# A four-layer model on one core: first weights loaded a stage ahead, a scatter moved over a stage boundary, B and C rows read from four copies

## Chip, cores, metric

The kernel runs on one core of one Trainium2 chip. The metric is the device time of one launch in microseconds (us), median of the runs.

## The reference

Four layers of an attention-like part and a feed-forward part, each followed by a residual sum and a layer norm, on a state of 2048 tokens by 1024 channels, in float32. Cut to the parts that the change touches:

```python
# layer 0, feed-forward: channels permuted, 16 small MLPs, permuted back
t = x.reshape(b*l, Dm)[:, perm].reshape(b*l, h, d)
t = gelu(einsum('bhd,hdm->bhm', t, up)); t = einsum('bhm,hmd->bhd', t, down)
x = layernorm(x + t.reshape(b*l, h*d)[:, unperm])
# layer 1, attention: a convolution of 3 taps gives q, k, v; attention in blocks of 128
c = conv(x, conv_w) + conv_b; q, k, v = split(c, 3)
qh, kh, vh = q@wq + bq, k@wk + bk, v@wv + bv            # 16 heads of 64
... softmax in each block ...; y = (o@wo + bo)@proj_w + proj_b
x = layernorm(x + y)
# layer 2, "attention": a selective scan, 2048 channels, 16 states
ssm_p = einsum('bdl,ed->ble', xc, x_proj_w)             # dt (64), B (16), C (16), each rms-normed
h = exp(dt*A)*h + dt*B_t*x_t                            # for each t, channel, state
y_t = sum over states of h*C_t
# layer 3, attention
qkv = x@Wqkv + bqkv                                     # 1024 -> 3*256
```

## The kernel before, in words

The state (`state`, `K.X`) stays in SBUF, channels on the partitions: 8 tiles (`KT`) of 128 channels by 2 x 1024 tokens. Work goes in chunks of 512 tokens (`NT`), of which there are 4 (`CHUNKS`). The program is a row of stages; each is a block in which the five instruction queues (SP for DMAs, POOL, TensorE, VectorE, ScalarE) run their own written-out order and meet by semaphores. Between blocks all engines meet. After a layer's part `recycle` (L68) clears the semaphores and all engines meet again. A stage's tiles and weights live in that stage alone, so each stage's SP queue starts with the loads of its own weights.

**Layer 0.** `l0_attn` (L1029) runs the attention, then one block for the output projection `L0Out` and the feed-forward `L0Ffn`. SP there loads `up`, `down` and then, as soon as a chunk has been scattered, that chunk back from DRAM (`Unpermute.load`, L1183). POOL first gathers the rows of the output weights (`l0out_rows`, L982), which TensorE turns (L996) before it can project. The permutation back is done by scatter: for each chunk eight indirect DMAs from POOL (`Unpermute.scatter`, L1176, issued at L1180) write the chunk's rows to DRAM in their final order. The scatter of chunk i waits for that chunk's last scaling (`ln.done`, VectorE L138). The last chunk's load stands in the convolution's SP queue.

**Convolution** (`conv`, L1203). 6 output tiles (m) times 2 batches give 12 units of 28 us. For each m SP loads the outer taps into `G` (L1235, L1236) and the middle tap into `mid` (L1239); ScalarE halves `mid` (L1270), VectorE adds the outer taps (L1288) and makes two more weight tiles (L1291, L1292). VectorE makes the input pieces `V` (L1302 to L1304), with a ring of 4, eight for a unit. TensorE multiplies at L1255, L1256 (outer taps) and L1260, L1261 (made tiles). Unit 1 needs chunks 2 and 3 of the state.

**Block attention** (`block_attention`, L1333). SP loads four biases (L1375) and `wq`, `wk`, `wv`, `wo` (L1376 to L1379), 1 MB each. TensorE waits for the biases, then for `wq`.

**Layer 2.** `l2_inproj` (L2251) projects and convolves; at its end the 128 rows of normed dt, B, C of each chunk (in `sq`) are stored to `l_ssm` in DRAM (L2295), and SP waits for these stores. `l2_scan` (L2477) goes through 4 chunks x 16 channel tiles (`ct`) = 64 items (q), each of 8 steps of two states. POOL makes `dtx*B` of a step (L2772, three steps ahead), VectorE scans (L2842), then the product with C is done by VectorE in five of eight steps (L2853) and by POOL in three (L2797). TensorE sums the states (L2676), and in between computes the gate (L2666) and the output projection of earlier chunks (L2463). B and C must lie on all 128 partitions: `rows` (L2582) loads two rows of one chunk from DRAM into `Bb` or `Cb` with a source that repeats for every partition, 512 KB a load, 16 loads a chunk. There is one buffer for a chunk's rows, so group g of chunk c+1 is loaded once the last item of chunk c has used group g.

**Layer 3.** `l3_project` (L3003): SP loads `W` in eight row blocks (L3019), the first tile waits for each of them (L3032).

Of the kernel before, what the change touches and what calls it, by code (L numbers as in the profile page):

```python
# [23 lines left out]
P = 128  # L24
# [1004 lines left out]
def l0_attn(nc, K, w, w_ffn, back):  # L1029
    with Stage(nc, "l0") as s:  # L1030
        o = Holder()
        o.oT = s.sb("oT", [P, GROUPS, T])
        with Stage(nc, "l0qkv") as s1:
            o.hi = s1.sb("hi", [P, 2, T], F32R)
            o.lo = s1.sb("lo", [P, 2, T], F32R)
            o.v = s1.sb("v", [P, T // P, HEADS, HP])
            a = L0Attn(nc, K, w)
            with Stage(nc, "l0proj") as s2:
                a.project(s2, o)
            with Stage(nc, "l0att") as s2:  # L1040
                a.attend(s2, o)
        with Stage(nc, "l0pair") as s1:
            pair = Pair(s1, K, 2, ())
            with Stage(nc, "l0out") as s2, Stage(nc, "l0ffn") as s3:
                pair.run(nc, L0Out(s2, K, w, o.oT, pair), L0Ffn(s3, K, w_ffn, back, pair))
# [17 lines left out]
class L0Ffn(DenseLN):  # L1063
# [6 lines left out]
    def __init__(self, s, K, w, back, pair):  # L1070
        super().__init__(s, K, pair=pair, first=CHUNKS, banks=slice(4, 6))
        self.w, self.back = w, back
# [9 lines left out]
    def sync(self, e):  # L1082
# [72 lines left out]

class Unpermute:
# [19 lines left out]
    def scatter(self, g, i, done, n):  # L1176
        g.wait_ge(self.rows_ok, CHUNKS)
        g.wait_ge(done, n)
        for k in range(KT):
# [23 lines left out]
def conv(nc, K, w, qkv, back):  # L1203
# [5 lines left out]
    with Stage(nc, "l1conv") as s:  # L1209
        G = s.sb("G", [P, 2, 4, KT, P])  # L1210
        mid = s.sb("mid", [P, KT, P])
# [6 lines left out]
        w_in = [s.sem(f"w_in{j}") for j in range(2)]  # L1218
        mid_in = s.sem("mid_in")
# [2059 lines left out]
```

## Time and profile before

| | |
|---|---|
| median of 3 runs | 5426.35 us (5425.6 to 5430.8) |
| the profiled execution | 5436.66 us |
| its span, first to last instruction | 5434.9 us |
| TensorE busy | 4925.0 us (91%) |
| VectorE busy | 3253.0 us (60%) |
| ScalarE busy | 2120.0 us (39%) |
| POOL busy | 2304.8 us (42%), nearly all of it in the scan, 2400 to 4330 us |
| mean granted TensorE clock | 0.953 |
| DMA | 358 MB, mean 66 GB/s |

A share over the whole span says little here, since the stages have different limits: each place that the change touches has to be read from its own stretch. Times in the rows are microseconds from the start of the span. PE is TensorE, DVE VectorE, ACT ScalarE, POOL GpSimd, SPq the queue of SyncE with the DMAs that it issues.

### The profile page before, as it was taken

The page shows a single profiled execution, that of the slowest core. Times are in us where ns is not written, and L with a number is a line of the kernel's source. Part 1 is how long each engine was busy: PE and PEld are TensorE (multiplying, and loading weights), DVE is VectorE, ACT ScalarE, POOL GpSimd, SP SyncE. Part 2 cuts the span into 40 slices and gives each one's busy share as a digit, 9 for nine tenths or more (in the row PEclk, how much of TensorE's full clock was granted, in tenths as well). Part 3 has the DMA queues.
Part 4 walks back from the last instruction along what each step waited for, and adds up shares of the span by engine and source line. Part 5 has one row for each costly group of instructions (what it writes and reads, how often), then busy time and mean ns, then how long its engine had stood idle before and what let it go on. Part 6 is the DMA issues. An engine that isn't in the chain of part 4 may idle for free. (4 is left out here: it accounts for less than half of the span.)

```text
span 5434.9 us, 40419 instructions
## 1 busy us (share of the span) xinstructions
PE 4925.0 (91%) x14496; PEld 2357.8 (43%) x14496; DVE 3253.0 (60%) x3534; ACT 2120.0 (39%) x2856; POOL 2304.8 (42%) x1219
## 2 busy tenths in 40 slices
PE   8998879989868899967888999999999999899998
PEld 4443224467626444423333444444344344456443
DVE  1663458845457323238998999899899822103522
ACT  1454620045333211135665666666566521102211
POOL 1003420000032100019998999999899842100421
PEclk9898989999979999988999999999999999999999
DMA  2001030000010022132116445544744320000001
GB/s 74 1 1 55 31 116 35 12 32 1 8 33 1 28 70 70 54 96 62 41 36 154 134 135 143 169 128 125 175 135 135 120 93 0 23 0 13 35 16 47
DMA packets 174758, 358.21 MB, mean 66 GB/s; under 512 B 18590, under 2 KB 52510, under 8 KB 170462
## 3 DMA queue, kind: packets, MB, share of 16 engines
q1 hardware_dynamic: 166494, 327.82, 20.2%
q0 software_dynamic: 8064, 27.80, 1.4%
q8 instruction: 116, 1.90, 0.1%
q14 instruction: 84, 0.69, 0.0%
HBM read 299.98 MB, written 55.57 MB: 65 GB/s over the span
## 5 line engine op out<-in xcount | busy, mean ns | idle before, releaser
L2772 POOL TENSOR_TENSOR l2scan_h<-l2scan_dtx,l2scan_Bb 128x1024 f32<-128x1024 f32 x512 | 1199.7, 2362 | 73.2 <-DMA l2scan_Bb<-l_ssm 56.7
L2676 PE MATMUL l2scan_yp<-l2scan_h,ident 128*128 128x512 f32 x2048 | 984.9, 615 | 134.6 <-POOL l2scan_h L2797 122.6
L2741 ACT ACTIVATE l2scan_ring<-l2scan_dt,l2scan_A 128x512 f32<-128x512 f32 x1024 | 661.3, 681 | 506.1 <-DVE l2scan_h L2853 399.6
L2676 PEld LDWEIGHTS l2scan_yp<-l2scan_h,ident 128*128 128x128 f32 x2048 | 393.1, 195 | 661.4 <-issue 486.4
L2666 PE MATMUL l2scan_low_z<-state,l2scan_Wz 128*128 128x512 f32 x1024 | 485.3, 607 | 3.5 <-DMA l2scan_Wz<-l_attn_in_z 3.5
L2797 POOL TENSOR_TENSOR l2scan_h<-l2scan_h,l2scan_Cb 128x1024 f32<-128x1024 f32 x192 | 452.7, 2358 | 11.0 <-DVE l2scan_h L2842 3.3
L2337 PE MATMUL l2in_acc<-state,l2in_W 128*128 128x512 f32 x1024 | 444.4, 594 | 11.5 <-DMA l2in_W<-l_attn_in_x 11.5
L2853 DVE TENSOR_TENSOR l2scan_h<-l2scan_ring,l2scan_Cb 128x1024 f32<-128x1024 f32 (+1 forms) x384 | 394.3, 1041 | 46.6 <-DMA l2scan_Cb<-l_ssm 41.4
L2842 DVE TENSOR_TENSOR_SCAN l2scan_ring<-l2scan_ring,l2scan_carry,l2scan_h 128x512 f32<-128x512 f32 x320 | 392.7, 1272 | 0.0
L2842 DVE TENSOR_TENSOR_SCAN l2scan_ring<-l2scan_ring,l2scan_h 128x512 f32<-128x512 f32 x320 | 373.3, 1212 | 10.3 <-POOL l2scan_h L2772 10.3
L2463 PE MATMUL l2scan_oacc<-l2scan_oy,l2scan_oW 128*128 128x512 f32 x768 | 353.2, 592 | 0.4 <-DMA l2scan_oy<-l_y 0.4
L2666 PEld LDWEIGHTS l2scan_low_z<-state,l2scan_Wz 128*128 128x128 f32 x1024 | 202.3, 198 | 268.2 <-issue 263.6
L2337 PEld LDWEIGHTS l2in_acc<-state,l2in_W 128*128 128x128 f32 x1024 | 194.2, 190 | 259.5 <-issue 247.1
L2392 DVE TENSOR_SCALAR l2in_cv<-l2in_xp,l2in_cw,l2in_cb 128x2048 f32<-128x2048 f32 (+1 forms) x17 | 21.8, 1284 | 395.9 <-ACT l2in_xc L2357 353.5
L2842 DVE TENSOR_TENSOR_SCAN l2scan_h<-l2scan_ring,l2scan_carry,l2scan_h 128x512 f32<-128x512 f32 x192 | 235.2, 1267 | 0.0
L2369 ACT ACTIVATE l2in_xp<-l2in_acc 128x512 f32<-128x512 f32 x64 | 38.3, 598 | 480.9 <-PE l2in_acc L2337 480.9
L2463 PEld LDWEIGHTS l2scan_oacc<-l2scan_oy,l2scan_oW 128*128 128x128 f32 x768 | 145.8, 190 | 184.6 <-issue 182.2
L2154 PE MATMUL l3pair_bank<-state,l3ffn_W 128*128 128x512 f32 x512 | 225.6, 593 | 0.0
L2842 DVE TENSOR_TENSOR_SCAN l2scan_h<-l2scan_ring,l2scan_h 128x512 f32<-128x512 f32 x192 | 223.4, 1204 | 2.8 <-POOL l2scan_h L2772 2.8
L2985 PE MATMUL l2pair_bank<-state,l2ffn_W 128*128 128x512 f32 x512 | 221.6, 592 | 0.0
L710 DVE TENSOR_REDUCE l0att_part<-l0att_SB 128x1 f32<-128x512 f32 x192 | 130.9, 690 | 72.5 <-PE l0att_SB L876 71.9
L147 POOL TENSOR_TENSOR l1proj_part<-l1proj_z 128x1024 f32<-128x1024 f32 x3 | 7.0, 2344 | 387.1 <-DVE l1proj_z L1661 387.1
(395 smaller groups left out, 7763.6 us busy)
## 6 DMA issues: line engine op xcount, KB each, us to landing
l2scan_oy<-l_y SPq DMA_DIRECT2D x192, 512.0 KB, 4.7
l2scan_Wz<-l_attn_in_z SPq DMA_DIRECT2D x64, 512.0 KB, 3.6
l2scan_oW<-l_attn_out_w SPq DMA_DIRECT2D x192, 128.0 KB, 3.1
l_xc<-l2in_xc SPq DMA_DIRECT2D x16, 1024.0 KB, 4.8
l2scan_xc<-l_xc SPq DMA_DIRECT2D x64, 256.0 KB, 5.2
l2scan_Bb<-l_ssm SPq DMA_DIRECT2D x32, 512.0 KB, 18.9
l2scan_Cb<-l_ssm SPq DMA_DIRECT2D x32, 512.0 KB, 24.8
l_y<-l2scan_zs SPq DMA_DIRECT2D x64, 256.0 KB, 4.9
```

The costliest lines, as they stand in the source:

```text
L710: v.tensor_reduce(part[:, H % 2, i // 2, i % 2:i % 2 + 1], SB[:, i % 2, :], AX.X, ALU.max, negate=True).then_inc(max_ok, 1)
L2154: t.matmul(acc, self.W[:, k, m * P:(m + 1) * P], x[:, k, :], start=k == 0, stop=False)
L2337: last = t.matmul(acc[:, n % 4, :], W[:, ct % 2, k, :], x[:, k, :], start=k == 0, stop=k == KT - 1)
L2463: last = t.matmul(self.acc, self.W[:, j, k], self.y[:, j, k], start=kp == 0 and k == 0, stop=kp == PIECES - 1 and k == PIECE - 1)
L2666: last = t.matmul(low_z[:, :], Wz[:, q % 2, k, :], x[:, k, :], start=k == 0, stop=k == KT - 1)
L2676: last = t.matmul(yp[:, :], K.ident[:, :], h[:, st % SLOTS, j, :], start=g == 0 and j == 0, stop=g == NSG - 1 and j == SGR - 1)
L2741: a.activation(bank(st, j), dt[:, q % 2, :], ACT.Exp, scale=A[:, ct, n:n + 1]).then_inc(dA_ok, 1)
L2772: g_.tensor_tensor(h[:, st % SLOTS], dtx[:, None, :].to_broadcast([P, SGR, NT]), Bb[:, g * SGR:(g + 1) * SGR, :], ALU.mult).then_inc(dBx_o ...
L2797: g_.tensor_tensor(hs, hs, Cb[:, g * SGR:(g + 1) * SGR, :], ALU.mult).then_inc(hC_g, 1)
L2842: last = v.tensor_tensor_scan(out, bank(st, j), hs[:, j, :], init, ALU.mult, ALU.add)
L2853: last = v.tensor_tensor(hs[:, js], src, Cb[:, g * SGR + js.start:g * SGR + js.stop, :], ALU.mult)
L2985: last = t.matmul(acc, self.W[:, k, m * P:(m + 1) * P], x[:, k, :], start=k == 0, stop=k == KT - 1)
```

## The change

- `Early`: two rooms of 16 KB a partition, one of them that of `oT`, which layer 0 is done with by then, and a tile `mid`, live from the L0 pair to the end of layer 1. The L0 pair's SP queue loads the convolution's first outer and middle taps there (three loads of 512 KB, behind `down`). The convolution uses the rooms as its two `G` buffers; at the end of its SP queue, once TensorE has used the tile of m=4, `wq` and `wk` go into the first room. `wv` and `wo` go into the second in the block attention's SP queue, as before.
- The last chunk's scatter moves from the L0 pair's POOL queue to the start of the convolution's; its load stands in front of m=1 on SP.
- The L1 projection has no z buffers of its own (`NZ = 0`) and writes into the state.
- The B and C rows (64 rows of a chunk, 128 KB) are stored four more times, into `l2_bc` (4, 64, T). `rows` loads each quarter of the partitions from its own copy: four loads of 128 KB for one of 512 KB; the waits count four times 16.
- `FirstTile`: the first 128 columns of `Wqkv` (512 KB) are loaded in the L2 pair's SP queue, last. The first projection tile uses them; the second waits for the row blocks of `W`.

```diff
 class L0Ffn(DenseLN):
     def sync(self, e):
         e.dma_start(self.down[:, :, :, :], self.w["down"]).then_inc(self.down_in, 16)
+        self.early.conv_tile(e)
         for i in range(CHUNKS - 1):
             self.back.load(e, i)
     def gpsimd_work(self, g):
             if i:
-                self.back.scatter(g, i - 1, self.ln.done, self.first + i)
-        for i in range(CHUNKS - 2, CHUNKS):
-            self.back.scatter(g, i, self.ln.done, self.first + i + 1)
+                self.back.scatter_after(g, i - 1, self.ln.done, self.first + i)
+        self.back.scatter_after(g, CHUNKS - 2, self.ln.done, self.first + CHUNKS - 1)
+class Early:
+    def conv_tile(self, e):
+        e.dma_start(self.G[0][:, 0], self.w["conv_w"][0, :, 0]).then_inc(self.g_in[0], 16)
+        e.dma_start(self.G[0][:, 3], self.w["conv_w"][0, :, 2]).then_inc(self.g_in[0], 16)
+        e.dma_start(self.mid[:, :, :], self.w["conv_w"][0, :, 1]).then_inc(self.mid_in, 16)
+
+    def qk_weights(self, e, v_used, n):
+        e.wait_ge(v_used, n)
+        e.dma_start(self.wq, self.w["wq"]).then_inc(self.wq_in, 16)
+        e.dma_start(self.wk, self.w["wk"]).then_inc(self.wk_in, 16)
...
 def conv(...):
                 e.dma_start(b[:, :], w["conv_b"]).then_inc(b_in, 16)
-                for m in range(M):
-                    if m == 1:
-                        back.load(e, CHUNKS - 1)
+                back.load(e, CHUNKS - 1)
+                for m in range(1, M):
                     if m >= 2:
                         e.wait_ge(v_used, KT * BATCH * (m - 1))
...
+                early.qk_weights(e, v_used, KT * BATCH * (M - 1))
+
+            @block.gpsimd
+            def _(g):
+                back.scatter(g, CHUNKS - 1)
...
 def block_attention(...):
-                e.dma_start(wq[:], w["wq"]).then_inc(wq_in, 16)
-                e.dma_start(wk[:], w["wk"]).then_inc(wk_in, 16)
-                e.dma_start(wv[:], w["wv"]).then_inc(wv_in, 16)
-                e.dma_start(wo[:], w["wo"]).then_inc(wo_in, 16)
+                e.dma_start(wv, w["wv"]).then_inc(wv_in, 16)
+                e.dma_start(wo, w["wo"]).then_inc(wo_in, 16)
...
 class L1Proj(ThinLN):
+    NZ = 0
...
+class FirstTile:
+    def __init__(self, s, src):
+        self.src = src
+        self.W = s.sb("W", [P, KT, P])
+        self.w_in = s.sem("w_in")
+    def load(self, e):
+        e.dma_start(self.W[:, :, :], self.src).then_inc(self.w_in, 16)
...
 def l2_inproj(...):
                     e.dma_start(ssm_dram[:, i * NT:(i + 1) * NT], sq[:, i, :]).then_inc(ssm_out, 16)
-                e.wait_ge(ssm_out, 16 * CHUNKS)
+                    for r in range(COPIES):
+                        e.dma_start(mem.bc[r][:, i * NT:(i + 1) * NT], sq[B_AT:P, i, :]).then_inc(ssm_out, 16)
+                e.wait_ge(ssm_out, 16 * CHUNKS * (1 + COPIES))
...
 def l2_scan(...):
                 def rows(dst, at, c, sem):
-                    src = ssm_dram[at:at + SGR, c * NT:(c + 1) * NT]
-                    e.dma_start(dst, src[None, :, :].to_broadcast([P, SGR, NT])).then_inc(sem, 16)
+                    for r in range(COPIES):
+                        src = mem.bc[r][at - B_AT:at - B_AT + SGR, c * NT:(c + 1) * NT]
+                        e.dma_start(dst[r * SHARE:(r + 1) * SHARE], src[None, :, :].to_broadcast([SHARE, SGR, NT])).then_inc(sem, 16)
...
 class L2Ffn(DenseLN):
     def sync(self, e):
             e.dma_start(self.W[:, k, :], self.w_rows[k * P:(k + 1) * P, :]).then_inc(self.w_in[k], 16)
+        self.lead.load(e)
...
 def l3_project(...):
+                        if n == 0:
+                            t.wait_ge(lead.w_in, 16)
                         for k in range(KT):
-                            if n == 0:
+                            if n == 1:
                                 t.wait_ge(w_in[k], 16)
-                            last = t.matmul(acc[:, n % 4, :], W[:, k, m * P:(m + 1) * P], x[:, k, :], start=k == 0, stop=k == KT - 1)
+                            Wm = lead.W[:, k, :] if m == 0 else W[:, k, m * P:(m + 1) * P]
+                            last = t.matmul(acc[:, n % 4, :], Wm, x[:, k, :], start=k == 0, stop=k == KT - 1)
```

`COPIES` is 4 and `SHARE` is 32.

## Rows read from the trace of the kernel before

**Rows 1.** Stages: us, busy by engine (x instructions), clock, DMA share, GB/s

```profile
2480.00:2860.00 380.00, 319.62 (x657) 131.12 (x656) 358.22 (x421) 249.56 (x341) 373.29 (x210) 0.91 0.14 40
2412.00:2452.00 40.00, 10.88 (x14) 4.20 (x14) 16.90 (x20) 17.02 (x24) 20.27 (x11) 0.59 0.79 166
1107.00:1117.00 10.00, 7.18 (x24) 6.04 (x25) 0.00 (x0) 2.37 (x5) 0.00 (x0) 0.66 0.95 399
```

**Rows 2.** The page's costliest groups: busy, mean ns, idle before, releaser

```profile
L2772 POOL TENSOR_TENSOR l2scan_h<-l2scan_dtx,l2scan_Bb 128x1024 f32<-128x1024 f32 x512 | 1199.7, 2362 | 73.2 <-DMA l2scan_Bb<-l_ssm 56.7
```

**Rows 3.** Order of time, L0 pair into convolution: start, us, instruction, [idle before]

```profile
732.83 4.42 DVE L138 TENSOR_TENSOR state<-l0pair_z,l0pair_stats 128x4096 f32<-128x4096 f32 x1 [9.16 <-ACT l0pair_stats L224]
738.00 0.97 POOL L1180 DMA_INDIRECT l_state_rows<-state,unperm_rows  x1 [21.52 <-DVE state L138]
...
746.93 0.97 POOL L1180 DMA_INDIRECT l_state_rows<-state,unperm_rows  x1 [0.30 <-issue]
753.29 1.23 DVE L1302 TENSOR_TENSOR l1conv_V<-state 128x1024 f32<-128x1024 f32 x1 [16.04 <-PEq L72]
758.65 1.22 DVE L1288 TENSOR_TENSOR l1conv_ends<-l1conv_G 128x1024 f32<-128x1024 f32 x1 [2.93 <-DMA l1conv_G<-l_attn_conv_w]
761.14 1.23 DVE L1291 SCALAR_TENSOR_TENSOR l1conv_G<-l1conv_ends,l1conv_mid 128x1024 f32<-128x1024 f32 x1 [1.27 <-ACT l1conv_mid L1270]
763.64 1.10 PE L1260 MATMUL l1conv_acc<-l1conv_V,l1conv_G 128*128 128x512 f32 x2 [1.25 <-DVE l1conv_G L1292]
l_state_rows<-state,unperm_rows POOLq DMA_INDIRECT x8, 2.7
state<-l_state_rows SPq DMA_DIRECT2D x1, 2048.0 KB, 10.3
```

**Rows 4.** The same view at the turn from layer 1's projection to its feed-forward

```profile
1597.31 0.48 DVE L1823 MEMSET l1ffn_router<- 128x512 f32 x1 [1.23 <-PEq L72]
```

**Rows 5.** Tile `l0out_rows`: us from issue to landing of its eight gathers

```profile
DMA to landing us min/median/max: 3.6/6.7/8.1
```

**Rows 6.** Order of time, start of the block attention, and a bias load's landing

```profile
1104.31 0.43 SPq L1375 DMA_DIRECT2D l1att_bo<-l_attn_bo  x1
1109.82 5.64 PE L1403 MATMUL l1att_pj<-l_qkv,l1att_wq 128*128 128x256 f32 x16 [10.46 <-DMA l1att_wq<-l_attn_wq]
l1att_bo<-l_attn_bo SPq DMA_DIRECT2D x1, 1.0 KB, 1.8
```

**Rows 7.** Order of time, start of the last projections, and a stretch of it

```profile
4715.13 0.33 SPq L3017 DMA_DIRECT2D l3proj_b<-l_attn_bqk  x1
4718.75 29.55 PE L3032 MATMUL l3proj_acc<-state,l3proj_W 128*128 128x512 f32 x64 [12.12 <-DMA l3proj_W<-l_attn_wqkv]
4727.80 0.69 ACT L3049 ACTIVATE l3qkv_qk<-l3proj_acc,l3proj_b 128x512 f32<-128x512 f32 x1 [18.58 <-PE l3proj_acc L3032]
4734.61 0.69 ACT L3049 ACTIVATE l3qkv_qk<-l3proj_acc,l3proj_b 128x512 f32<-128x512 f32 x1 [6.12 <-PE l3proj_acc L3032]
4718.70:4724.00 5.30, 5.25 (x9) 2.19 (x10) 0.00 (x0) 0.00 (x0) 0.00 (x0) 0.72 0.96 350
```

**Rows 8.** Order of time, stores before the scan and the scan's first issues

```profile
2396.68 2.29 SPq L2295 DMA_DIRECT2D l_ssm<-l2in_sq  x4
2401.74 0.32 SPq L2580 DMA_DIRECT2D l2scan_ssm<-l_ssm  x1
...
2404.47 0.43 SPq L2584 DMA_DIRECT2D l2scan_Bb<-l_ssm  x1
2415.97 4.64 POOL L2772 TENSOR_TENSOR l2scan_h<-l2scan_dtx,l2scan_Bb 128x1024 f32<-128x1024 f32 x2
```

**Rows 9.** Order of time, SP at the change to chunk 1

```profile
2889.30 1.76 SPq L2584 DMA_DIRECT2D l2scan_Bb<-l_ssm  x3
...
2909.14 5.48 SPq L2584 DMA_DIRECT2D l2scan_Bb<-l_ssm  x1
2923.38 2.82 SPq L2567 DMA_DIRECT2D l2scan_Wz<-l_attn_in_z  x1
```

More of the change, by code:

```diff
@@ L1026, with l0_attn, l0_out_ffn @@
 class Holder: pass
[L1029 to L1045, printed above, removed]
+def l0_attn(nc, K, w, oT):
+    o = Holder()
+    o.oT = oT
+    with Stage(nc, "l0qkv") as s1:
+        o.hi = s1.sb("hi", [P, 2, T], F32R)
+        o.lo = s1.sb("lo", [P, 2, T], F32R)
+        o.v = s1.sb("v", [P, T // P, HEADS, HP])
+        a = L0Attn(nc, K, w)
+        with Stage(nc, "l0proj") as s2:
+            a.project(s2, o)
+        with Stage(nc, "l0att") as s2:
+            a.attend(s2, o)
+def l0_out_ffn(nc, K, w, w_ffn, oT, back, early):
+    with Stage(nc, "l0pair") as s1:
+        pair = Pair(s1, K, 2, ())
+        with Stage(nc, "l0out") as s2, Stage(nc, "l0ffn") as s3:
+            pair.run(nc, L0Out(s2, K, w, oT, pair), L0Ffn(s3, K, w_ffn, back, early, pair))
 def host_l0attn(i, x):
@@ L1068, with __init__ @@
     MT = M // P
-    def __init__(self, s, K, w, back, pair):
+    def __init__(self, s, K, w, back, early, pair):
         super().__init__(s, K, pair=pair, first=CHUNKS, banks=slice(4, 6))
-        self.w, self.back = w, back
+        self.w, self.back, self.early = w, back, early
         self.up = s.sb("up", [P, KT, self.M])
@@ L1153, in scalar, with __init__ @@
         self.ln.a_std(a, self.first + CHUNKS - 1)
+class Early:
+    def __init__(self, s, w, room):
+        self.w = w
+        other = s.sb("room", [P, 4 * D])
+        self.G = tuple(x.rearrange("p (f k n) -> p f k n", f=4, k=KT) for x in (other[:, :], room))
+        self.mid = s.sb("mid", [P, KT, P])
+        halves = lambda x: (x[:, 0:2 * D].rearrange("p (k n) -> p k n", k=WK), x[:, 2 * D:])
+        self.wq, wk = halves(other[:, :])
+        self.wk = wk.rearrange("p (k n) -> p k n", k=WK)
+        self.wv, wo = halves(room)
+        self.wo = wo.rearrange("p (k n) -> p k n", n=W3)
+        self.g_in = [s.sem(f"g_in{j}") for j in range(2)]
+        self.mid_in = s.sem("mid_in")
+        self.wq_in, self.wk_in = s.sem("wq_in"), s.sem("wk_in")
+    def conv_tile(self, e):
[6 more added lines that the diff above has]
+        e.dma_start(self.wk, self.w["wk"]).then_inc(self.wk_in, 16)
 class Unpermute:
@@ L1200, with conv @@
 MASKED = -1.0e9
-def conv(nc, K, w, qkv, back):
+def conv(nc, K, w, qkv, back, early):
     M = 3 * W3 // P
@@ L1209, in conv @@
     with Stage(nc, "l1conv") as s:
-        G = s.sb("G", [P, 2, 4, KT, P])
-        mid = s.sb("mid", [P, KT, P])
+        G, mid = early.G, early.mid
         ends = s.sb("ends", [P, KT, P])
@@ L1217, in conv @@
         acc = s.ps("acc", [P, 2, 4, HALF])
-        w_in = [s.sem(f"w_in{j}") for j in range(2)]
-        mid_in = s.sem("mid_in")
+        w_in, mid_in = early.g_in, early.mid_in
         b_in = s.sem("b_in")
@@ L1342, in block_attention @@
     with Stage(nc, "l1att") as s:
-        wq, wk, wv = (s.sb(n, [P, WK, HW]) for n in ("wq", "wk", "wv"))
-        wo = s.sb("wo", [P, HW // P, W3])
+        wq, wk, wv, wo = early.wq, early.wk, early.wv, early.wo
         bq, bk, bv = (s.sb(n, [P, HW // P]) for n in ("bq", "bk", "bv"))
@@ L1359, in block_attention @@
         b_in = s.sem("b_in")
-        wq_in, wk_in, wv_in, wo_in = (s.sem(n) for n in ("wq_in", "wk_in", "wv_in", "wo_in"))
+        wq_in, wk_in = early.wq_in, early.wk_in
+        wv_in, wo_in = s.sem("wv_in"), s.sem("wo_in")
         mask_ok = s.sem("mask_ok")
@@ L2937, in l2_attn @@
         with Stage(nc, "l2out") as s1, Stage(nc, "l2ffn") as s2:
-            pair.run(nc, L2Out(s1, K, w, y_dram, pair), L2Ffn(s2, K, ffn_rows, w_ffn["bias"], pair))
+            pair.run(nc, L2Out(s1, K, w, mem.y, pair), L2Ffn(s2, K, mem.rows, w_ffn["bias"], lead, pair))
 def host_l2attn(i):
@@ L2958, with __init__ @@
 class L2Ffn(DenseLN):
-    def __init__(self, s, K, w_rows, bias, pair):
+    def __init__(self, s, K, w_rows, bias, lead, pair):
         super().__init__(s, K, pair=pair, first=CHUNKS, banks=slice(0, 4))
```

94 lines of the change are left out of this document (55 added, 39 removed).

## The prediction

> **What bounds the kernel now.** I read four views in this order. First the busy time by stage: in a steady stretch of the scan (380 us of chunk 0) POOL works 373.29 us and VectorE 358.22 us, so whatever holds POOL up in the scan is paid in full [rows 1]. The 210 POOL instructions there are 16 per item (8 products, 3 more for the groups of kind W with 3 copies, 2 small ones), so 13.1 items of 29.0 us. Second the page's row for POOL's product `dtx*B`: 512 of 2.362 us, 73.2 us idle before them, 56.7 of it until a load of `Bb` lands [rows 2]. Third the order in time at the four places where stages meet that the change touches. At the end of layer 0 VectorE's last scaling ends at 737.25 (732.83+4.42), POOL then issues eight scatters until 747.90, and VectorE's first instruction of the convolution stands at 753.29, after 16.04 us idle [rows 3]. Elsewhere a turn between stages costs VectorE 1.23 us [rows 4]. TensorE waits for first weights at the start of the block attention and of the last projections [rows 6, 7]. Fourth the issues of SP and the DMA rate in the scan [rows 1, 8, 9]: while B and C rows are loaded the DMA engines are 79% busy but move 166 GB/s, against 399 GB/s at 95% when ordinary weights are loaded. So the broadcast load, not SP or the engines' number, is slow.
>
> **The change part by part.**
>
> *Last scatter and first weights of the convolution.* The L0 pair's block no longer ends with POOL's eight scatters. It ends with VectorE at 737.25, and with the ordinary turn of 1.23 us the convolution's first VectorE instruction goes to 738.5: 14.8 us earlier. The bound from the other side is the turn that follows POOL here, 747.90 to 753.29, 5.4 us: then only 10.6 us. I take 14.8, since POOL's previous scatters end 20 us before. Inside the block VectorE waits 2.93 us for `G` and 1.27 us for the halved `mid` before it can build the tap weights; both tiles are there now, so TensorE's third kind of product (763.64) comes another 4.2 us earlier, at 744.6 [rows 3]. Part: -19.0 (-14.8 to -19.0). What is late next: the scatters now run beside the convolution's first unit. They start at 738.5, the last is issued 8.9 us later (746.93 less 738.00) and lands 2.7 us after that, at 750.1. SP holds the chunk's load until then, and behind it on SP stand `G` and `mid` of m=1. The load took 10.3 us with 1 MB in front of it, so 760.4. VectorE first asks for it before unit 1, which it cannot reach before TensorE has used five pieces of unit 0. The remaining covers are over 10 us, because TensorE wants that unit only after its 28 us of unit 0. Weights of m=1, 1.5 MB more, land some 4 us later and are needed after that. So nothing; if the cover were gone, each us late would cost one.
>
> *Price of the early loads.* SP issues 1.5 MB more (three loads) at the start of the L0 pair, behind `up` and `down`, beside the gathers of `l0out_rows` that TensorE turns one by one. These take 3.6, 6.7 and 8.1 us to land (least, median, most). If the late ones took the most instead of the median, the last tiles would come 1.4 us later. The lower end is 0, since TensorE and ScalarE take the later gathers one by one and may be behind them anyway. I take 0.8 [rows 5]. The loads of chunks behind them on SP wait for scatters over 200 us later. One 0.5 MB load on SP at the end of the L2 pair's weights is over 270 us ahead of its use: nothing. In place of three z buffers the L1 projection writes into the state with the same instructions; its only wait that goes (slot reuse at chunk 3) had long been met: nothing.
>
> *Block attention.* `wq`, `wk` go into the first tile buffer once TensorE has used the tile of m=4, a whole tile (over 50 us) before the end. TensorE still waits for the four bias loads: the last is issued at 1104.31 and lands after 1.8 us, 1106.1. It started at 1109.82. Part: -3.7. `wv` and `wo` move forward on SP by two issues and are needed later than that [rows 6].
>
> *Last projections.* TensorE starts when the block does, 4715.3, instead of 4718.75: -3.5. The first tile lasted 9.05 us to its eviction, the second 6.81, so 2.2 us of it were waits for the eight row blocks or the low clock (granted 0.72 on the mean in these 5.3 us, so part of them at 1.2 GHz and not 2.4, after TensorE had stood idle). The low clock stays, the waits go, so -3.5 to -5.7; I take -3.5. The second tile takes the waits on `W`, which by then has landed [rows 7].
>
> *B and C rows, the stores.* In the tail of the input projection SP issues 4 stores; now 20, one after another. Six issues from 2401.74 to 2404.47 give 0.455 us each, so 16 more cost 7.3 us, and all engines wait for the last to land before the scan begins: +7.3. From 6 (pitch 0.37) to 9 (if 3 MB of stores back up) [rows 8].
>
> *B and C rows, the loads.* 256 loads of 128 KB in place of 64 of 512 KB. No row shows such a load from four places. If the rate goes up, SP's 0.455 us becomes the limit: 1.82 us a group, 288 GB/s; a group of 512 KB at 166 GB/s now takes 3.2 us. Start of the scan, counted from SP's first issue: the eighth B group is issued as numbers 65 to 68 of the queue, 30.9 us, and lands near 34; POOL wants it at about 36.7 (first product at 14.2 as now, 2415.97 less 2401.74, seven products, two W products and a 1.26 us sum). Change of a chunk: now SP spends 2889.30 to 2923.38, 34.1 us, on the 16 loads; 64 at 0.455 are 29.1, so what stands behind them on SP (`Wz`, the store of y, the next loads) is not later [rows 9]. POOL takes a new group every 3.6 us, SP delivers a B and a C group in 3.64. So of the 56.7 us I leave 2 standing: -54.7. The other end is 0, if the rate stays at 166 GB/s.
>
> Why I expect the rate to rise: at 166 GB/s the engines are four fifths busy, so their packets are stretched; what is special is that 128 reads go to the same 4 KB. Four copies spread them only so far as the 16 queues are at different loads at one time. A load (128 KB in runs of 2 KB over 16 queues) now gives each queue 4 packets instead of 16, and a lag of a few packets between queues suffices. Weights from many addresses run at 399 GB/s [rows 1].
>
> The Trainium skill, page "DMA: Bandwidth & Descriptors", section "Rules for kernel authors", speaks against it: two transfers to disjoint partition halves serialize on the same 16 engines, so one should be used. By that rule the split itself gains nothing, and the sum would be that of the first rival below.
>
> **The sum.** -19.0 +0.8 -3.7 -3.5 +7.3 -54.7 = -72.8 us. The profiled execution took 5436.66 us (span 5434.9, 1.8 around it) and would take 5363.9. It stands 10.3 us (0.2%) above the median of the runs, so the median goes from 5426.35 to 5353.5.
>
> **The rivals.**
> 1. *The copies do not spread.* All 16 queues work on the same copy at a time, or the four copies, 512 KB apart, answer as slowly as one. For it: the rate stayed near 166 GB/s over whole bursts in which B and C rows of different addresses were queued [rows 1, 9]. Then POOL's 56.7 us stay and the stores' 7.3 are lost: -25.4+7.3 = -18.1, 5408. The skill's page "DMA: Bandwidth & Descriptors", section "Latency and other measured facts", reports rates that fall at large power-of-two row pitches, unharmed at 512 KiB; by it this rival would not hold, and no run here shows it.
> 2. *Half way.* The rate reaches about 200 GB/s, 2.6 us a group: the late groups of each burst still come a few us late, some 6 us for each of four bursts: -25.4+7.3-31 = -49, 5377.
> 3. *Slower than before.* SP becomes the bound of the scan: an issue costs not 0.455 but what it costs behind a full queue (up to 5.48 us a load in a burst now [rows 9]). Place: the 64 issues of each burst. At the present rate a group takes 3.2 us, so the new loads break even at 0.8 us each; the whole change turns slower from 0.8+18.1/256 = 0.87 us. At 1.0: 256 x 0.2 = +51, 51-18 = +33, 5459. Against it: the long issues scale with the packets that must drain, and a quarter of a load has a quarter of them.
> 4. *The change of the convolution's start does nothing,* because the scatter now gates unit 1. It would need the load to land 12 us later than worked out; with the scan's gain in full the result is near 5370, and it stays inside the range.
>
> **How the numbers follow.** Forecast 5353.5: chance 0.60 (5338 to 5366 with the ends of its terms). Rival 1: 0.14. Rival 2: 0.14. Rival 3: 0.06. Rival 4: 0.02. Several small losses together, near no change: 0.04. For 8 in 10 the range must take in rival 2 and reach rival 1: 5338 to 5410. A measurement here can tell about 0.2%, 11 us, from no change. Rival 1 at 18 us loses that margin when the convolution's turn and the stores are at their worse ends; I give 0.03 of its 0.14 to "within". Faster: 0.60+0.14+0.02+0.11 = 0.87. Within: 0.03+0.04 = 0.07. Slower: 0.06.
>
> **What would show it.** In the profile after: VectorE's first instruction of the convolution about 1.2 us after the last scaling, the scatters behind it, no idle time before its weights, and none before unit 1; TensorE's first query about 3.7 us after the biases are issued; the first projection at the block's start; 20 stores over 9 us before the scan; in the scan POOL's idle time on `Bb` near 2 us instead of 56.7 and a DMA rate well above 166 GB/s in the bursts with SP's issues 0.46 us apart. It is wrong if that rate stays at 166 GB/s (then 5408), or if issues take a us each in the bursts (then slower).

## The result, and the profile after

| | before | after |
|---|---|---|
| median of the runs | 5428.6 us (5425.6 to 5437.4) | 5380.6 us (5372.2 to 5387.5) |
| ratio | | 0.9912, 95% interval 0.9895 to 0.9929 |
| profiled execution, its span | 5436.7, 5434.9 us | 5376.3, 5374.5 us |
| POOL idle until `Bb` lands | 56.7 us | 14.8 us |

The change made the kernel faster by 48 us by the medians; the forecast was 73, and the range held the result. The two profiled executions differ by 60.4 us. A second measurement of the changed kernel, in one session with later experiments, gave 0.9897 (0.9880 to 0.9914). Of the runs below, one of the kernel with the copies outside took 7124 us at a granted clock of 0.69, beside 5549 to 5562 us in its five others, and is left out of its ratio.

First the page of the changed kernel: its rows for POOL's product `dtx*B` and VectorE's `h*C` (busy, mean ns, idle before, releaser), and the two kinds of loads (count, KB, median us to landing). The last row is VectorE's `h*C` on the page of the kernel before.

```profile
L2838 POOL TENSOR_TENSOR l2scan_h<-l2scan_dtx,l2scan_Bb 128x1024 f32<-128x1024 f32 x512 | 1199.5, 2361 | 30.3 <-DMA l2scan_Bb<-l_bc 14.8
L2919 DVE TENSOR_TENSOR l2scan_h<-l2scan_ring,l2scan_Cb 128x1024 f32<-128x1024 f32 (+1 forms) x384 | 394.5, 1041 | 6.4 <-DMA l2scan_Cb<-l_bc 1.0
l2scan_Bb<-l_bc SPq DMA_DIRECT2D x128, 128.0 KB, 6.9
l2scan_Cb<-l_bc SPq DMA_DIRECT2D x128, 128.0 KB, 7.7
L2853 DVE TENSOR_TENSOR l2scan_h<-l2scan_ring,l2scan_Cb 128x1024 f32<-128x1024 f32 (+1 forms) x384 | 394.3, 1041 | 46.6 <-DMA l2scan_Cb<-l_ssm 41.4
```

The first row answers to [rows 2]: the waits went from 56.7 to 14.8 us, not to the 2 of the forecast. VectorE's waits for `Cb` went from 41.4 to 1.0 us. The reason stands in the stretch of the scan's first burst (15 us from 4 us after SP's first `Bb` load; us, busy by engine, clock, DMA share, GB/s):

```profile
2394.96:2409.96 15.00, 3.48 (x4) 1.34 (x5) 6.49 (x8) 9.59 (x14) 9.29 (x5) 0.50 1.07 224
```

The rate rose from 178 GB/s (the same 15 us of before; 166 over the 40 us of [rows 1]) to 224 and no further, though SP, at 1.84 us for four loads, offers 285. The DMA engines are now busy all the time: the share is 1.07, and was 0.80 in these 15 us of before.

Second the order of time where the L0 pair meets the convolution, against [rows 3]:

```profile
732.11 4.42 DVE L138 TENSOR_TENSOR state<-l0pair_z,l0pair_stats 128x4096 f32<-128x4096 f32 x1 [9.33 <-ACT l0pair_stats L224]
738.10 1.23 DVE L1336 TENSOR_TENSOR l1conv_V<-state 128x1024 f32<-128x1024 f32 x1 [1.57 <-PEq L72]
738.64 1.54 POOL L1213 DMA_INDIRECT l_state_rows<-state,unperm_rows  x1 [23.04 <-POOLq L72]
740.45 1.22 DVE L1322 TENSOR_TENSOR l1conv_ends<-early_room 128x1024 f32<-128x1024 f32 x1
744.22 1.10 PE L1294 MATMUL l1conv_acc<-l1conv_V,early_room 128*128 128x512 f32 x2 [1.33 <-DVE early_room L1326]
...
753.37 2.04 POOL L1213 DMA_INDIRECT l_state_rows<-state,unperm_rows  x1 [0.30 <-issue]
757.18 0.36 SPq L1218 DMA_DIRECT2D state<-l_state_rows  x1
765.16 1.23 DVE L1336 TENSOR_TENSOR l1conv_V<-state 128x1024 f32<-128x1024 f32 x1 [4.71 <-DMA state<-l_state_rows]
766.66 0.19 PEld L1289 LDWEIGHTS l1conv_acc<-l1conv_V,early_room 128*128 128x128 f32 x1 [0.24 <-DVE l1conv_V L1336]
```

VectorE begins 1.57 us after the last scaling instead of 16.04, and has no wait before the weights. The eight scatters end at 755.4, not at the 747 of the forecast, and VectorE waits 4.71 us for the chunk. TensorE comes to unit 1 at 766.66, with the 0.24 us between weight loads that it has anyway, and the piece was ready at 766.39. So the scatters cost nothing, by 0.3 us. That is in part luck: the chunk's load was there 8.0 us after its issue (757.18 to 765.16), and with the 10.3 us that it took in the kernel before, TensorE would have waited some 2 us.

Third the starts of the block attention and the last projections, against [rows 6, 7]:

```profile
1084.89 0.43 SPq L1409 DMA_DIRECT2D l1att_bo<-l_attn_bo  x1
1086.73 5.59 PE L1435 MATMUL l1att_pj<-l_qkv,early_room 128*128 128x256 f32 x16 [6.79 <-DMA l1att_bo<-l_attn_bo]
...
4656.78 0.33 SPq L3079 DMA_DIRECT2D l3proj_b<-l_attn_bqk  x1
4656.84 7.40 PE L3097 MATMUL l3proj_acc<-state,l3first_W 128*128 128x512 f32 x12 [8.71 <-PEq L72]
4666.05 0.69 ACT L3114 ACTIVATE l3qkv_qk<-l3proj_acc,l3proj_b 128x512 f32<-128x512 f32 x1 [15.34 <-PE l3proj_acc L3097]
```

In the block attention TensorE starts 1.84 us after the last bias load's issue instead of 5.51. In the last projections it starts with the block (0.06 us behind SP's first issue) instead of 3.6 us into it.

Fourth SP before the scan, against [rows 8]:

```profile
2373.46 0.32 SPq L2357 DMA_DIRECT2D l_ssm<-l2in_sq  x1
2373.83 2.41 SPq L2359 DMA_DIRECT2D l_bc<-l2in_sq  x4
...
2383.03 2.55 SPq L2359 DMA_DIRECT2D l_bc<-l2in_sq  x4
2388.23 0.32 SPq L2645 DMA_DIRECT2D l2scan_ssm<-l_ssm  x1
```

From the first store to the scan's first load it takes 14.77 us; before it took 5.06. A store of a copy costs SP 0.61 us, not 0.46. [Rows 8] had a nearer price than that of the loads: the four stores of before took SP 2.29 us, 0.57 each.

### The profile page after: what moved, and what is told of

Same layout as the page of the kernel before. It is cut to its first block and busy times, and to the rows that moved or that the text cites. A ratio compares the mean times of both kernels' runs of the same rounds, so it can differ in the third digit from the quotient of the medians.

```text
span 5374.5 us, 40636 instructions
## 1 busy us (share of the span) xinstructions
PE 4917.7 (91%) x14496; PEld 2354.3 (44%) x14496; DVE 3253.8 (61%) x3534; ACT 2119.0 (39%) x2856; POOL 2311.0 (43%) x1219
## 5 line engine op out<-in xcount | busy, mean ns | idle before, releaser
L2838 POOL TENSOR_TENSOR l2scan_h<-l2scan_dtx,l2scan_Bb 128x1024 f32<-128x1024 f32 x512 | 1199.5, 2361 | 30.3 <-DMA l2scan_Bb<-l_bc 14.8
```

The source lines that it names most:

```text
L2838: g_.tensor_tensor(h[:, st % SLOTS], dtx[:, None, :].to_broadcast([P, SGR, NT]), Bb[:, g * SGR:(g + 1) * SGR, :], ALU.mult).then_inc(dBx_o ...
```

## The experiments

The question was where the scan's gain stopped: 46.1 us came out of 54.7. The table has all runs in the order in which they were made. *Tail* is the time from the first store of the input projection's tail to the scan's first load. *Scan* is the time from POOL's first product of `dt` and `x` to its last. Rate and share are those of 15 us from 4 us after the first `Bb` load, as above.

| kernel | ratio to before (interval) | tail | scan | GB/s | share |
|---|---|---|---|---|---|
| before | 1 | 5.1 | 1875.4 | 178 | 0.80 |
| changed kernel | 0.9912 (0.9895 to 0.9929) | 14.8 | 1829.3 | 224 | 1.07 |
| four loads, one place | 0.9970 (0.9959 to 0.9981) | 14.6 | 1873.6 | 157 | 0.79 |
| partitions interleaved | 0.9920 (0.9906 to 0.9933) | 14.7 | 1836.3 | 208 | 0.78 |
| copies 520 KB apart | one run, 5380.9 us | 14.7 | 1829.1 | 239 | 1.06 |
| no copies | 0.9961 (0.9947 to 0.9975) | 5.1 | 1876.1 | 179 | 0.92 |
| scatter in the pair | 0.9915 (0.9902 to 0.9928) | 14.6 | 1830.6 | 234 | 1.06 |
| one load, copies outside | 1.0222 (1.0208 to 1.0235) | 14.7 | 2003.4 | 115 | 0.31 |
| one load, copies inside | 0.9860 (0.9845 to 0.9874) | 14.7 | 1813.6 | 396 | 1.02 |
| one store a chunk | 0.9888 (0.9871 to 0.9905) | 14.6 | 1830.8 | 233 | 1.07 |
| changed kernel again | 0.9897 (0.9880 to 0.9914) | 14.7 | 1832.8 | 236 | 1.06 |
| one load, one copy | 0.9852 (0.9836 to 0.9869) | 7.1 | 1811.0 | 388 | 1.02 |
| one load, two copies | 0.9857 (0.9832 to 0.9882) | 9.9 | 1812.3 | 386 | 1.01 |
| copies made late | 0.9847 (0.9832 to 0.9862) | 7.6 | 1812.1 | 397 | 1.01 |

**Four loads from one place.** Do the copies matter, or only the split into four loads?

```diff
-                        src = mem.bc[r][at - B_AT:at - B_AT + SGR, c * NT:(c + 1) * NT]
+                        src = mem.bc[0][at - B_AT:at - B_AT + SGR, c * NT:(c + 1) * NT]
```

> The changed kernel, but all four loads of 32 partitions read the same copy; the stores of all four copies stay, so only where the loads read from differs. Theory A (128 reads of one 4 KB place are what holds the rate at 166 GB/s, and four places spread them): the rate of the bursts falls from 229 back to about 166 GB/s, POOL's idle time on Bb goes from 14.8 us back to 57 or more, the time rises by 40 to 50 us to about 5425. Theory B (the split into four loads alone gives the rate, the copies do nothing): 229 GB/s, 15 us on Bb, the same time as the changed kernel within 10 us (5380).

```profile
2401.78:2416.78 15.00, 2.98 (x4) 1.25 (x5) 6.34 (x8) 9.73 (x14) 7.16 (x4) 0.50 0.79 157
L2838 POOL TENSOR_TENSOR l2scan_h<-l2scan_dtx,l2scan_Bb 128x1024 f32<-128x1024 f32 x512 | 1198.5, 2359 | 72.5 <-DMA l2scan_Bb<-l_bc 54.4
```

The stretch and the page's row: 157 GB/s, 54.4 us on `Bb`, 5422 us. With these loads (runs of 2 KB, 32 partitions) the copies are what helps, and the split alone does nothing. Theory A held here.

**Interleaved partitions.** Does it matter which partitions a load fills?

```diff
-                        e.dma_start(dst[r * SHARE:(r + 1) * SHARE], src[None, :, :].to_broadcast([SHARE, SGR, NT])).then_inc(sem, 16)
+                        e.dma_start(dst[r::COPIES], src[None, :, :].to_broadcast([SHARE, SGR, NT])).then_inc(sem, 16)
```

> The changed kernel, but load r fills partitions r, r+4, r+8 and so on instead of 32 neighbouring ones; copies, sizes and number of loads stay. Theory C (229 GB/s is the limit of loads that write 32 neighbouring partitions, since these reach only part of the ways into SBUF): the rate rises to what SP's pitch of 0.46 us allows, about 280 GB/s, landing stays near 4 to 5 us through the burst, POOL's idle time on Bb falls from 14.8 to under 5 us and the time by 8 to 10 us, to about 5371. Theory D (the limit is on the side that is read, four places for 128 reads): 229 GB/s, 15 us on Bb, no change of the time beyond 5 us (5380).

The stretch, SP's issues, and the page's row of the loads:

```profile
2394.52:2409.52 15.00, 3.36 (x4) 1.27 (x5) 6.36 (x8) 9.72 (x14) 8.58 (x5) 0.50 0.78 208
2393.18 2.53 SPq L2650 DMA_DIRECT2D l2scan_Cb<-l_bc  x4
l2scan_Bb<-l_bc SPq DMA_DIRECT2D x128, 128.0 KB, 3.1
```

The time is about the same (scan 1836.3 us against 1829.3 and 1832.8), yet neither theory gives it. What theory C says of the cause fits, its rate and time do not. A load lands in 3.1 us instead of 6.9 and the engines are busy 0.78 of the time instead of 1.07, so the limit of the changed kernel, that its loads fill neighbouring partitions, is gone. But such a load costs SP 0.63 us instead of 0.46: 512 KB in 2.53 us is 207 GB/s, and that is the rate. SP has become the limit, and POOL waits 18.6 us for `Bb`. The Trainium skill, page "SBUF — State Buffer", section "Door 1: The DMA port swizzle (why `[64,N]` ≈ `[32,N]`)", says that 32 neighbouring partitions reach 8 of 16 ports and at most some 218 GB/s. The 224 to 239 GB/s at a full share in the changed kernel lie somewhat above that. There, loads for all four quarters of the partitions were under way one behind the other; no row here shows a port.

**Copies 520 KB apart.** The tensor of the copies got 65 rows a copy instead of 64.

> The changed kernel, but the four copies lie 520 KB apart instead of 512 KB (one row of padding between copies). Theory E (copies a power of two apart answer partly as one place, so that 229 GB/s is what is left): the rate rises above 250 GB/s and POOL's idle time on Bb falls from 14.8 us to under 8. Theory D or C: 229 GB/s and 15 us as before.

It took 5380.9 us, POOL waited 13.1 us for `Bb`, and the rate was 239 GB/s (236 in the second run of the changed kernel). So the copies' distance of 512 KB is not the limit.

**No copies.** Rows stored once and loaded as before; the two other parts stay.

```diff
-                    for r in range(COPIES):
-                        src = mem.bc[r][at - B_AT:at - B_AT + SGR, c * NT:(c + 1) * NT]
-                        e.dma_start(dst[r * SHARE:(r + 1) * SHARE], src[None, :, :].to_broadcast([SHARE, SGR, NT])).then_inc(sem, 16)
+                    src = ssm_dram[at:at + SGR, c * NT:(c + 1) * NT]
+                    e.dma_start(dst, src[None, :, :].to_broadcast([P, SGR, NT])).then_inc(sem, 16)
```

> The changed kernel with the B and C rows stored once and loaded as before (one load of 512 KB a group); the two other parts stay (last scatter and first weights of the convolution, early weights of block attention and last projections). If the parts add up as read from the two traces: the stores' 9.7 us go, the scan's 47.8 come back, so +38 us on the changed kernel and about -22 us on the kernel before, near 5405 (ratio 0.996), scan's start 9.7 us earlier than in the changed kernel, POOL's idle time on Bb near 57 us. Rival (the three early loads' gain is given back in the scan, or the change of phase is what costs): within 5 us of the kernel before, 5426.

```profile
L2835 POOL TENSOR_TENSOR l2scan_h<-l2scan_dtx,l2scan_Bb 128x1024 f32<-128x1024 f32 x512 | 1199.1, 2360 | 73.1 <-DMA l2scan_Bb<-l_ssm 56.1
```

The ratio is the one expected, 0.9961, with 56.1 us on `Bb`. So the early weights and the scatter are worth 21 us, and the copies the other 27 (by 0.9912) to 35 us (by 0.9897, the second measurement). The tail and the scan of the traces give 37 (46.8 less 9.7). The parts add up within these intervals.

**The scatter stays in the L0 pair.**

```diff
-        self.back.scatter_after(g, CHUNKS - 2, self.ln.done, self.first + CHUNKS - 1)
+        for i in range(CHUNKS - 2, CHUNKS):
+            self.back.scatter_after(g, i, self.ln.done, self.first + i + 1)
...
-            @block.gpsimd
-            def _(g):
-                back.scatter(g, CHUNKS - 1)
```

> The changed kernel, but the last eight scatters are issued by POOL at the end of the L0 pair again, as before the change; the early weights stay. Theory (POOL's scatters and the longer turn behind them are the 14.8 us of the start of the convolution; the early weights are the other 4.2): in this run's trace VectorE's first piece V comes about 16 us after the end of the last scaling plus the scatters, that is near 753, TensorE's third kind of product about 6 us after that instead of 10, the rest of the kernel unchanged, the time +14 to +16 us on the changed kernel (about 5395). Rival (the scatters only move their cost to a later wait in the convolution): +0 to +5 us.

The order of time at the turn:

```profile
730.39 4.42 DVE L138 TENSOR_TENSOR state<-l0pair_z,l0pair_stats 128x4096 f32<-128x4096 f32 x1 [7.63 <-ACT l0pair_stats L224]
744.51 0.97 POOL L1214 DMA_INDIRECT l_state_rows<-state,unperm_rows  x1 [0.30 <-issue]
751.01 1.23 DVE L1333 TENSOR_TENSOR l1conv_V<-state 128x1024 f32<-128x1024 f32 x1 [16.20 <-PEq L72]
753.35 1.22 DVE L1319 TENSOR_TENSOR l1conv_ends<-early_room 128x1024 f32<-128x1024 f32 x1
757.12 2.05 PE L1291 MATMUL l1conv_acc<-l1conv_V,early_room 128*128 128x512 f32 x2 [0.98 <-DVE early_room L1323]
```

VectorE's idle time is 16.20 us again instead of 1.57, and its first piece comes 14.6 us later after the last scaling than in the changed kernel (20.62 less 5.99); so does TensorE's third kind of product (26.73 less 12.11). The weights are there at once. The median is 14.2 us above that of the run with one store a chunk, which shared its session and whose tail and scan are those of the changed kernel; the runs of the two spread over 13 and 20 us, so the medians say that there is a cost and only roughly how much. Against the changed kernel's own ratios, from other sessions, the difference is 2 to 10 us; the medians of the kernel before itself lay between 5426 and 5439 us in the sessions, so only runs of one session should be set against each other at this size.

**One load of 128 partitions from the four copies,** copies outside or inside. For this the memory is laid out by chunk, so that a group's two rows lie side by side.

```diff
-        self.bc = nc.dram_tensor("l2_bc", (COPIES, P - B_AT, T), F32, kind="Internal").ap()
+        self.bc = nc.dram_tensor("l2_bc", (COPIES, CHUNKS, P - B_AT, NT), F32, kind="Internal").ap()
...
+                    src = mem.bc[:, c, at - B_AT:at - B_AT + SGR].rearrange("r s n -> r (s n)")
+                    e.dma_start(dst.rearrange("p s n -> p (s n)"), src[None].to_broadcast([SHARE, COPIES, SGR * NT])).then_inc(sem, 16)
```

This is the form with the copies inside (the waits for `Bb` and `Cb` count one DMA a group again); outside, the source is `src[:, None, :].to_broadcast([COPIES, SHARE, SGR * NT])`.

> The changed kernel, but each group is loaded by one DMA of 128 partitions: its source counts through the four copies (copies outside, 32 equal reads inside), with the two rows of a group side by side in memory for that. Bytes, copies and stores stay; SP issues 64 loads instead of 256. Theory P (229 GB/s is the limit of loads that each write 32 neighbouring partitions): the rate goes up, above 260 GB/s over a burst, POOL's idle time on Bb falls from 14.8 to under 5 us, the time by about 10 us to near 5370. Theory D (four places give 229 GB/s and no more): rate and time as in the changed kernel (5380). Theory Q (with one DMA all 16 queues stay in step on one or two copies): back towards 166 GB/s, time near 5420.

> As the run with one DMA of 128 partitions from four copies, but with the copies inside: partition p reads copy p modulo 4. Theory Q (queues in step meet on the same copy): slower than with the copies outside, towards 166 GB/s and 5420. Theory P: the same as with the copies outside, above 260 GB/s and near 5370.

The stretch with the copies outside:

```profile
2397.40:2412.40 15.00, 0.00 (x0) 0.00 (x0) 5.03 (x6) 9.72 (x14) 4.87 (x3) 0.50 0.31 115
```

The stretch with the copies inside, and its page row for POOL's product:

```profile
2383.11:2398.11 15.00, 3.32 (x4) 1.26 (x5) 6.35 (x8) 9.71 (x14) 9.91 (x6) 0.50 1.02 396
L2837 POOL TENSOR_TENSOR l2scan_h<-l2scan_dtx,l2scan_Bb 128x1024 f32<-128x1024 f32 x512 | 1199.1, 2361 | 14.3 <-PE l2scan_yp L2741 8.6
```

The same 64 loads of the same bytes run at 115 or at 396 GB/s, by the order of two dimensions. Theory Q expected the copies inside to be the slower of the two; it is the other way round, and for another cause than engines that meet on one copy: the share is 0.31, so most engines had nothing to do. The Trainium skill, page "DMA: Bandwidth & Descriptors", section "Rules for kernel authors", says that an outermost dimension under 16 confines a DMA to at most that many engines; 4 of 16 is 0.25. The trace agrees: in the 8 us from 2425 the share is 0.26 at 104 GB/s, and over the 15 us above, where other transfers ran beside the loads, 0.31. No row names the engines here. With the copies inside, POOL doesn't wait for `Bb` at all, and theory P has its time nearly right (near 5370 expected, 5358 measured).

**One store a chunk for all four copies.**

```diff
-                    for r in range(COPIES):
-                        e.dma_start(mem.bc[r][:, i * NT:(i + 1) * NT], sq[B_AT:P, i, :]).then_inc(ssm_out, 16)
+                    e.dma_start(mem.bc[:, :, i * NT:(i + 1) * NT].rearrange("r p t -> p r t"), sq[B_AT:P, i, None, :].to_broadcast([P - B_AT, COPIES, NT])).then_inc(ssm_out, 16)
```

> The changed kernel, but the four copies of a chunk are stored by one DMA that reads the rows four times, not by four DMAs: 8 stores in the tail of the input projection instead of 20. Theory I (the tail's 9.7 us are SP's issues, 0.6 us each): 12 issues fewer give 7 us back, the scan's first issue comes 7 us earlier after l2's last scaling, the time is about 5373. Rival W (the tail is the writing of 2.5 MB or the landing of the last store): less than 3 us back.

```profile
2378.57 0.65 SPq L2358 DMA_DIRECT2D l_bc<-l2in_sq  x1
...
2382.61 2.29 SPq L2358 DMA_DIRECT2D l_bc<-l2in_sq  x1
...
2385.82 2.27 SPq L2358 DMA_DIRECT2D l_bc<-l2in_sq  x1
2392.84 0.32 SPq L2644 DMA_DIRECT2D l2scan_ssm<-l_ssm  x1
```

Rival W held. There are 8 stores instead of 20, but the last two of the copies keep SP 2.3 us each, and the tail is 14.63 us instead of 14.77. What the tail costs goes with the amount that is stored, not with the number of issues: 1 MB takes 5.1 us (before), 1.5 MB 7.1 and 7.6, 2 MB 9.9 and 3 MB 14.6 to 14.8 (later runs included).

**The changed kernel once more,** as the base of the last session.

> The changed kernel itself once more, as the point that the other runs of this call are compared with (the medians of the kernel before lay 10 us apart between calls). If the parts add up as the traces have them, it lies 35 to 40 us below the run without copies, that is at a ratio of 0.989 to the kernel before; if the ratio of its first runs, 0.991, stands, the copies bring only 27 us and 10 us of the scan's gain are given back somewhere.

It is at 0.9897, its median 5380.7 us. The interval (0.9880 to 0.9914) holds both 0.989 and 0.991, so this run doesn't decide between the two cases.

**One copy, and two, with one load inside.** Against the kernel with the copies inside, only the number of copies changes.

```diff
-COPIES = 4
+COPIES = 1
```

> One DMA of 128 partitions a group with the group's two rows side by side (reads of 4 KB), but one copy only: all 128 partitions read the same 4 KB; 8 stores in the tail. Theory A (reads of one place hold the rate): 166 GB/s, POOL's idle time on Bb near 57 us, a time of 5405 to 5412, as the run without copies. Rival L (the longer reads of 4 KB, not the copies, made the run with copies inside fast): 288 GB/s, no idle time on Bb, 5351.

> As before it, with two copies (partition p reads copy p modulo 2), 12 stores in the tail. Theory A with rate in proportion to places until something else limits: between 230 and 288 GB/s, POOL's idle time on Bb under 10 us; with 8 stores fewer than four copies have (4 to 5 us) the time is 5353 to 5360. If two copies give only 166 to 200 GB/s: 5375 to 5400.

The stretch and POOL's product with one copy:

```profile
2388.66:2403.66 15.00, 3.02 (x3) 1.00 (x4) 6.06 (x7) 9.72 (x14) 9.61 (x6) 0.50 1.02 388
L2837 POOL TENSOR_TENSOR l2scan_h<-l2scan_dtx,l2scan_Bb 128x1024 f32<-128x1024 f32 x512 | 1198.1, 2359 | 13.2 <-PE l2scan_yp L2741 7.4
```

The stretch with two copies:

```profile
2391.70:2406.70 15.00, 3.50 (x4) 1.34 (x5) 6.51 (x8) 9.58 (x14) 10.05 (x6) 0.50 1.01 386
```

This overturned theory A as a general rule, and rival L held for the time (5351 expected, 5355 measured). With one copy all 128 partitions read the same 4 KB, as before the change, and the rate is 388 GB/s. The number of copies (1, 2, 4) changes nothing beyond the tail: 388, 386, 396. Two copies took 5357.6 us, inside the 5353 to 5360 expected, though the rate is above the 230 to 288 GB/s of that sum. Against the run without copies, what differs in the load is only that its two rows are one run of 4 KB and not two of 2 KB, 8 KB apart. That alone gives what the copies gave and the rest besides: scan 1811.0 us instead of 1876.1.

The packets' own durations in these traces (20 us of each burst, from 4 us after the first `Bb` load; median, and in brackets the middle half) show the three cases:

```
                              GB/s  share  packets of 2 KB        packets of 4 KB
before                         172   0.85  162 ns (84 to 192)
no copies                      169   0.94  175 ns (84 to 193)
four loads, one place          158   0.84  165 ns (84 to 192)
changed kernel                 225   1.06  149 ns (141 to 158)
partitions interleaved         208   0.77   84 ns (84 to 84)
one load, one copy             393   1.02   84 ns (others)        160 ns (159 to 166)
```

Most 2 KB packets take 84 ns in the run with interleaved partitions. From one place they fall into two groups, 0.3 to 0.4 of them under 100 ns and about as many between 175 and 210. With copies in the changed kernel nearly all take about 149, now because of the neighbouring partitions; without these they are at 84 with SP as the limit. A packet of 4 KB takes 160 ns, from one place or not: twice the bytes in about the time of a median packet of the kernel before. A single load with copies inside and reads of 2 KB was not tried.

**Copies made late.** Four copies, one load inside; of the copies only chunk 0's are stored in the tail.

```diff
-                    for r in range(COPIES):
+                    for r in range(COPIES if i == 0 else 0):
...
+                    if 2 <= q < 2 + CHUNKS - 1:
+                        i = q - 1
+                        src = ssm_dram[B_AT:P, i * NT:(i + 1) * NT]
+                        e.dma_start(mem.bc[:, i].rearrange("r p t -> p r t"), src[:, None, :].to_broadcast([P - B_AT, COPIES, NT])).then_inc(bc_out, 16)
```

> Four copies, one DMA of 128 partitions a group (partition p reads copy p modulo 4), and only chunk 0's copies stored in the tail of the input projection; those of chunks 1 to 3 are made inside the scan by three DMAs from memory to memory, behind the stores of items 1 to 3 on SP, over 300 us before their use. The tail has 8 stores instead of 20. Theory (the tail's 9.7 us follow the stores, 12 of the 16 added ones go): scan's first issue 6 to 8 us earlier than with all stores in the tail, nothing lost in the scan, ratio to the kernel before 0.9848 (about 5351 where the other had 5358). Rival (copies from memory to memory disturb the loads of the items beside them): POOL or VectorE idle at items 2 to 5, gain under 3 us.

```profile
2363.01 2.40 SPq L2359 DMA_DIRECT2D l_bc<-l2in_sq  x4
2365.46 1.57 SPq L2357 DMA_DIRECT2D l_ssm<-l2in_sq  x3
2370.21 0.33 SPq L2646 DMA_DIRECT2D l2scan_ssm<-l_ssm  x1
```

The tail falls from 14.7 to 7.6 us and the scan loses nothing (1812.1 against 1813.6): 0.9847, 5349.9 us, the fastest median. It can't be told from one copy (5355.2) by the intervals, and one copy is the simpler kernel. Both are about 25 to 31 us faster than the changed kernel of the same session (5380.7). One copy with its rows for chunks 1 to 3 stored late was not tried.

## Why the prediction was right, and where it was off

The range held the result because it took in rival 2. The measured 5380.6 us lies outside the 5338 to 5366 us that the forecast gave to its own terms, and 4 us from rival 2 (5377, chance 0.14), whose mechanism, a rate that rises only half way, is also the one that the traces show: 224 GB/s, where the forecast had 288 and rival 2 200.

The median came out 27 us above the forecast. Of these, 2 are the median of before (5428.6 in the new runs, not 5426.4), and 12.5 that the profiled execution of before stood 8 us above its median and that of after 4 us below. These 12.5 us lie within the spread between runs of one kernel and are no step of the working. The other 12.4 are the terms of the sum (72.8 forecast, 60.4 in the traces):

- **Start of the convolution, -19.0 with +0.8 for the early loads.** Measured -19.4 at TensorE's third kind of product (763.64 to 744.22). The last scaling came 0.7 us earlier, not 0.8 later, so the early loads cost nothing that shows. The run with the scatter in the pair gives 14.6 us for the scatter alone, by its trace.
- **The scatter beside unit 0.** The conclusion held, the working didn't: an issue takes 2.03 us beside VectorE's pieces, not 0.97, so the load was issued at 757.2 and not at 750.1. The wait that this gave (4.71 us, on VectorE) used up the cover to 0.3. The cover was never over 10 us: by the prediction's own numbers TensorE reaches unit 1 about 28 us after 739.7, and a chunk that lands at 760.4 gives a piece at 761.6, which leaves 6 us. Rival 4 asked for 12 us more before anything is lost and was far nearer than its chance of 0.02 said.
- **Block attention -3.7:** measured 3.67 (5.51 to 1.84 us after the last bias).
- **Last projections -3.5:** measured 3.25 from the last scaling to the first exponential of the attention (182.75 to 179.50 us). The first eviction stands 9.2 us behind TensorE's start, before 9.1, so leaving out the waits for row blocks gave no faster first tile. The granted clock over these stretches was 0.78 and 0.84 before; time times clock gives 7.6 us before and 7.2 after, so as an estimate the waits had cost 0.4 us, which the longer low clock took back.
- **Stores +7.3:** measured 9.7. The price of an issue was taken from loads (0.455), and a store costs 0.61. The amount stored is behind it, as the run with one store shows; the high end of 9 named that case and was still 0.7 short.
- **Loads -54.7:** measured 46.1 from the first item to the last. This is the step that failed most. The claim "if the rate goes up, SP's 0.455 us becomes the limit" left out that a load of 32 neighbouring partitions has a limit of its own: 224 to 239 GB/s at a full share, between the forecast (288) and rival 2 (200). POOL's 14.8 us on `Bb` are what is left. POOL's wait fell by 41.9 us. The scan gained 4.2 us more than that; VectorE's wait for `Cb`, 40 us shorter, stands in no term of the sum, and no run shows what it is worth by itself.
- These make -62.8. The other 2.4 us of the traces' difference were lost around the last layer normalisation of layer 2 and in the last attention; no run was made for them.

Why I expected the rate to rise was right for the loads as they are (four loads, one place: 157 GB/s), but "128 reads go to the same 4 KB" was not the whole cause: with the two rows side by side, 128 reads of one 4 KB run at 388 GB/s. Rival 1 fell, in both its forms: the copies spread, and 520 KB between them did no better than 512. The passage on row pitches that the prediction took from the Trainium skill bears on the second form alone. By the rule of the Trainium skill that the prediction quotes, a split gains nothing; the split alone indeed gained nothing (157 GB/s), so the trace agrees, and the gain was that of the addresses. Rival 3 did not come: the four issues took 1.84 us in the middle of bursts.

## What to carry to other kernels

When a broadcast load runs at half the rate of an ordinary one, first make each read longer (rows that are loaded together side by side in memory) before adding copies: here that gave 388 GB/s against 224, with fewer issues and fewer stores. Split a load over partitions only with its own limits in mind, those of 32 neighbouring partitions (224 to 239 GB/s) and of SP's issues, and keep the small dimension of the copies inside (outermost it gave 115 GB/s, inside 396). A stage's last DMA issues by POOL are worth moving into the next stage if the first unit there hides them, but count them at their price beside VectorE.

## What the runs showed of the hardware

- Reads of one place: at 2 KB each, the median packet takes 162 to 175 ns over 20 us and the rate is 157 to 179 GB/s; at 4 KB each, 160 ns and 388. Whether length, number of reads, or the 8 KB between the two rows is the cause is open; I didn't separate them.
- POOL's indirect DMA takes 0.97 us to issue in the kernel before, also beside VectorE's 4.4 us scaling (661.5 to 666.0), and 2.03 us beside VectorE's pieces, whose two operands lie in SBUF; the one issued at 742.82, as VectorE's last weight product began, took 0.97. Beside these pieces its period is 2.33 us, the period of VectorE's pieces (2.34). That the two hold each other up was not tested further.
- An issue by SP, with the gap behind it, costs 0.46 us for neighbouring partitions, 0.63 for every fourth, about 0.64 for one load that counts through copies, about 0.48 for the one with one copy, and 0.61 for a store of a copy in the tail.
- Behind POOL's scatters the turn to the next stage takes 5.5 us (745.48 to 751.01 in the run with the scatter in the pair; 5.4 in the kernel before). Without them VectorE's whole idle time is 1.57.
- Two profiled executions whose code is the same up to the tail reached it 13 us apart (2361.7 and 2374.8), with TensorE's granted clock at 0.92 and 0.89 in the first 500 us. That is the size of the spread between runs of one kernel here.
